# An adaLN block (state-space mixer and quantised feed-forward): decays in two half-chunk buffers, W_out in high and low parts, new orders

## The reference, cut to what matters

```python
zxbcdt = h @ W_in.T                          # z 1024, x 1024, B 128, C 128, dt 16
xBC = silu(conv4(xBC) + b_conv)
dt = softplus(dt_raw + dt_bias);  A = -exp(A_log)
# _ssd, per chunk, S is the state carried on:
L = exp(where(tril, cs[l] - cs[s], 0)) * tril       # cs = cumsum(dt * A)
Y_diag = (C B^T * L) X ;  Y_off = (C S) * exp(cs)
S = S * exp(cs_last) + B^T (X * exp(cs_last - cs))
y = (Y + Dp * X) * silu(z);  y = rmsnorm(y) * norm_w;  out = y @ W_out.T
# feed-forward: down(silu(gate(x)) * up(x)), weights (wq - 128) * scale
```

## Time and profile before

| what | us |
|---|---|
| median of 3 runs (1432.05 to 1432.34) | 1432.11 |
| profiled execution, span | 1430.4 |
| TensorE busy in it | 1408.2 (98%) |
| VectorE busy in it | 1143.5 (80%) |
| ScalarE busy in it | 641.9 (45%) |
| mixer and drain, until the feed-forward is alone | about 950 |

### The profile page before, as it was taken

How to read it: one execution, slowest core, us unless ns; L and a number is a source line. 1 busy time by engine, 2 the same in 40 slices (tenths; PEclk the granted TensorE clock), 3 DMA queues, 4 the chain that set the end, 5 groups by cost and what they waited for, 6 DMA issues and landing times.

```text
span 1430.4 us, 25660 instructions
## 1 busy us (share of the span) xinstructions
PE 1408.2 (98%) x9433; PEld 1134.0 (79%) x9433; DVE 1143.5 (80%) x2521; ACT 641.9 (45%) x1300; POOL 286.0 (20%) x335
## 2 busy tenths in 40 slices
PE   7999999999999999999999999899999999999998
PEld 3778787887887887887887887679888888888887
DVE  5799999999999999999999999856646546464542
ACT  5656566565565576476565565322202112020110
POOL 1012222223213213213212212221010211102101
PEclk9999999999999999999999999999999999999999
DMA  9413213213213213122222133612120201202010
GB/s 338 144 52 120 97 38 134 97 38 134 104 46 134 77 58 113 67 97 104 72 100 97 63 110 114 241 45 78 48 88 0 89 22 67 76 13 89 8 52 31
DMA packets 56411, 125.01 MB, mean 87 GB/s; under 512 B 6438, under 2 KB 10066, under 8 KB 52188
## 3 DMA queue, kind: packets, MB, share of 16 engines
q1 hardware_dynamic: 55744, 123.27, 24.2%
q10 hardware_dynamic: 540, 0.07, 0.0%
HBM read 97.62 MB, written 25.69 MB: 86 GB/s over the span
## 4 chain that ended last, share of the span: by engine, by line
PE 40%; DVE 37%; issue 15%; ACT 5%; DMA 1%; POOL 1%; DVEq 0%; POOLq 0%; SPq 0%; ACTq 0%
PE bank L2055 18%; DVE xBC L994 11%; PE bank L2085 9%; DVE decay L1069 6%; PE bank L1461 5%; DVE decay L1086 3%; DVE y L1142 2%; ACT decay L782 2%; DVE state L1129 2%; DVE X L1104 2%; PE bank L333 2%; DVE X_D L1135 1%; DVE y L1121 1%; PE bank L1617 1%; DVE bn_stats L965 1%
## 5 line engine op out<-in xcount | busy, mean ns | idle before, releaser
L994 DVE SCALAR_TENSOR_TENSOR xBC<-conv_in,wconv,xBC 128x256 f32<-128x256 f32 x480 | 240.8, 526 | 5.2 <-ACT xBC L709 4.3
L1890 ACT ACTIVATE silu_gate<-bank,params 128x512 f32<-128x512 f32 (+1 forms) x99 | 63.5, 642 | 372.0 <-PE bank L2055 352.5
L1962 DVE SCALAR_TENSOR_TENSOR hidden<-bank,params,silu_gate 128x512 f32<-128x512 f32 (+1 forms) x99 | 68.3, 690 | 129.2 <-PE bank L2055 124.1
L618 POOL TENSOR_TENSOR X_D<-X,Drow 128x1024 f32<-128x1024 f32 x32 | 65.7, 2052 | 388.1 <-ACT X_D L793 316.9
L2085 PE MATMUL bank<-W_down,hidden_high 128*128 128x512 f32 x374 | 138.9, 390 | 0.0
L2055 PE MATMUL bank<-ff_h_high,W_gate 128*128 128x512 f32 (+1 forms) x352 | 132.1, 379 | 0.0
L2055 PE MATMUL bank<-ff_h_high,W_up 128*128 128x512 f32 (+1 forms) x352 | 130.9, 376 | 0.4 <-DVE hidden L1962 0.4
L2055 PE MATMUL bank<-ff_h_low,W_gate 128*128 128x512 f32 (+1 forms) x352 | 130.9, 376 | 0.0
L2055 PE MATMUL bank<-ff_h_low,W_up 128*128 128x512 f32 (+1 forms) x352 | 130.9, 376 | 0.0
L2085 PE MATMUL bank<-W_down,hidden_low 128*128 128x512 f32 x330 | 128.4, 389 | 0.0
L1461 PE MATMUL bank<-h_high,W_in_high 128*128 128x256 f32 x640 | 126.5, 319 | 0.7 <-ACT z_dt L732 0.6
(11 more groups left out here) (194 smaller groups left out, 3183.9 us busy)
## 6 DMA issues: line engine op xcount, KB each, us to landing
decay<-sums_scratch SPq DMA_DIRECT2D x32, 1024.0 KB, 4.8
wq_rows<-wqT SPq DMA_DIRECT2D x33, 256.0 KB, 4.1
widened_scratch<-wq_rows SPq DMA_DIRECT2D x33, 256.0 KB, 2.0
x_tile<-x SPq DMA_DIRECT2D x32, 256.0 KB, 3.0
x_resid<-x SPq DMA_DIRECT2D x32, 256.0 KB, 2.8
x_scratch<-x_resid SPq DMA_DIRECT2D x32, 256.0 KB, 2.2
ff_x_resid<-x_scratch SPq DMA_DIRECT2D x32, 256.0 KB, 4.5
out<-ff_x_resid SPq DMA_DIRECT2D x32, 256.0 KB, 2.0
```

Of the source, the lines that this page charges most:

```text
L618: nc.gpsimd.tensor_tensor(A.XD[:].rearrange("p (h d) -> p h d", h=H), A.X[:].rearrange("p (h d) -> p h d", h=H), A.Drow[:].unsqueeze(2).br ...
L994: nc.vector.scalar_tensor_tensor(A.xc[b][:, m, :], A.raw[:, m, j:j + SC], A.wconv[:, m, j:j + 1], A.xc[b][:, m, :], ALU.mult, ALU.add).the ...
L1890: self.nc.scalar.activation(B.sg[m % 2][:, 0:size], self.gates[m % 2][:, 0:size], ACT.Silu, scale=self.T.sgate[:, m:m + 1]).then_inc(self. ...
L1962: nc.vector.scalar_tensor_tensor(hid, self.ups[m % 2][:, 0:size], self.T.sup[:, m:m + 1], B.sg[m % 2][:, 0:size], ALU.mult, ALU.mult).then ...
```

## The change

- Decays. One buffer `A.decay` in two halves `A.L[f]` of eight heads in the place of two chunk buffers. Each holds the heads f of chunk 0 and then of chunk 1. So the DMA for chunk 1 (`spread_sums`, 512 KB each) can be issued only when `y_diag(n, u, 0, f)` has read chunk 0, and `exp_decay(u, 1, f)` moves from the end of one turn into the middle of the next. In `drain` these DMAs are issued by ScalarE.
- `diff` is gone from VectorE. `exp_decay` makes it with eight `Relu(sum - x)` of 128x128 and then `Exp(-x)` on 1024 columns.
- W_out: `KF` = 7 tiles the split way and one plain. `evac_g` and `low_g` are made in two pieces each, `evac_g_last` copies the last tile.
- Work on a state that is zero (`fresh`: units 0 and 1, chunk 0) and on a state that nobody reads (`final`: units 14 and 15, chunk 1) is left out.
- Setup: the four matmuls of a section go to four groups of 32 columns of the array (`tile_position=(0, 32*k)`) without accumulation, and `turn_cols` adds the four groups by a matmul with `pick`.
- The orders of all engines are written anew; the residual of chunk 0 stands ahead of `rstd_next` on GpSimdE.

```diff
-        for k in range(self.T.DI // P - KH):
+        act.wait_ge(self.wout_in, 16 * (KF + 1))
+        for k in range(self.T.DI // P - KF):
...
-            mm = self.nc.tensor.matmul(self.mod_bank[s], self.A.sc[:, k, :], self.wm[s][:, k, :],
-                                       start=(k == 0), stop=(k == KD - 1))
+            g = self.GROUP * k
+            mm = self.nc.tensor.matmul(self.mod_bank[s][g:g + self.GROUP, :], self.wide_c[:, k, :], self.wm[s][k // 2][:, k % 2, :],
+                                       start=True, stop=True, tile_position=(0, g))
...
-            mm = self.nc.tensor.transpose(self.cols[s][:, k, :], self.mod_rows[s % 2][:, k * P:(k + 1) * P],
-                                          A.ident[0:2, 0:2])
+            mm = self.nc.tensor.matmul(self.cols[s][:, k, :], self.mod_rows[s % 2][:, k * P:(k + 1) * P], A.pick[:],
+                                       start=True, stop=True)
...
+    def fresh(u, c):
+
+        return u < 2 and c == 0
+
+    def final(u, c):
+
+        return u >= N - 2 and c == NC - 1
...
+    def spread_sums(queue, u, c, f):
+
+        if c:
+            wait(queue, ydiag_done, u, 2 * NC, f + 1)
+        else:
+            wait(queue, ydiag_done, u, 2 * NC, f + 1 - NC)
+        queue.dma_start(A.L[f].rearrange("p h l -> p (h l)"),
+                        T.cs_d[c].rearrange("h l -> (h l)")[f * HH * P:(f + 1) * HH * P]
+                        .rearrange("(a x) -> a x", a=1).broadcast_to([P, HH * P])).then_inc(cs_in[f], 16)
...
         def exp_decay(u, c, f):
+            wait(act, cs_in[f], u, 16 * NC, 16 * (c + 1))
+            if c == 0 and f == 0:
+
+                wait(act, sums_step, u, 3, 3)
+            x = A.L[f]
+            for h in range(HH):
+                o = c * H + f * HH + h
+                last = nc.scalar.activation(x[:, h, :], x[:, h, :], ACT.Relu, bias=A.s3[:, o:o + 1], scale=-1.0)
+            last.then_inc(diff_done, 1)
             wait(act, diff_done, u, 2 * NC, 2 * c + f + 1)
-            x = A.L[c][:, f * HH:(f + 1) * HH, :]
-            nc.scalar.activation(x, x, ACT.Exp).then_inc(decay_done, 1)
+            nc.scalar.activation(x, x, ACT.Exp, scale=-1.0).then_inc(decay_done, 1)
...
-            for h in range(f * HH, (f + 1) * HH):
-                last = nc.vector.tensor_scalar(A.L[c][:, h, :], A.L[c][:, h, :], A.s3[:, c * H + h:c * H + h + 1],
-                                               0.0, ALU.subtract, ALU.min)
...
-            for wp, gp in sorted(PARTS, key=lambda part: part[1]):
-                if gp == 1:
-                    wait(pe, glo_done, u, NC, c + 1)
-                for k in range(KH):
-                    nc.tensor.matmul(ps[:], gT[gp][:, k, :], Wo[wp][:, k, :],
-                                     start=(k == 0 and wp == gp == 0), stop=False)
+            halves = (range(0, 4), range(4, KF))
+            for f in range(2):
+                wait(pe, ghi_done, u, 2 * NC, 2 * c + f + 1)
+                for w in range(2):
+                    for k in halves[f]:
+                        nc.tensor.matmul(ps[:], A.gThi[:, k, :], Wo[w][:, k, :], start=(k == 0 and w == 0), stop=False)
+            for f in range(2):
+                wait(pe, glo_done, u, 2 * NC, 2 * c + f + 1)
+                for k in halves[f]:
+                    nc.tensor.matmul(ps[:], A.gTlo[:, k, :], A.Wohi[:, k, :], start=False, stop=False)
```

More of the change, by code:

```diff
@@ L67 @@
     ROWS = 3
+    GROUP = 32
     def __init__(self, nc, T, A, sem):
@@ L703, in evac_tile @@
             ps = a_wait(act, a_filled, n, ("m", m), 1)
+            if n == 0 and m == 0:
+                act.wait_ge(setup.mod_done, 2)
             wait(act, tail_step, n, 2, 0)
-            wait(act, yoff_done, before(n), 2 * NC, 0)
+            wait_for(act, yoff_done, yoff_count(before(n), 0) if n else 0)
             nc.scalar.activation(A.raw[:, m, 3:3 + SC], ps[:, 0:SC], ACT.Copy)
@@ L883, in turn @@
             if own:
-                silu_tile(n, b, 1)
+                evac_tile(n, b, 5)
+            if bef:
+                exp_decay(u, 1, 1)
+            if own:
                 evac_tile(n, b, 6)
@@ L1124, in decay_S @@
         def decay_S(u, b, c, f):
-            if u != N - 1 or c == 0:
-                wait(dve, yoff_done, u, 2 * NC, 2 * c + f + 1)
+            if not final(u, c) and not fresh(u, c):
+                wait_for(dve, yoff_done, yoff_count(u, 2 * c + f + 1))
                 wait(dve, e3_done, u, 1, 1)
@@ L1163, in low_g @@
+        def low_g(n, u, c, f):
+            wait(dve, ghi_done, u, 2 * NC, 2 * c + f + 1)
+            ps = t_wait(dve, t_filled, n, ("g", c, f), 1)
+            k = min(4 * f + 4, KF)
+            nc.vector.tensor_tensor(A.gTlo[:, 4 * f:k, :].rearrange("p k t -> p (k t)"), ps[:, 0:(k - 4 * f) * P],
+                                    A.gThi[:, 4 * f:k, :].rearrange("p k t -> p (k t)").bitcast(F32),
                                     ALU.subtract).then_inc(glo_done, 1)
@@ L1659, in turn @@
                 scores_G(n, u, b)
+                y_off(u, b, 0, 0)
             if own:
@@ L1694, in turn @@
                 transpose_g(n, u, 0, 0)
+                y_diag(n, u, 1, 0)
                 transpose_g(n, u, 0, 1)
+                y_off(u, b, 1, 0)
             if own:
@@ L1698, in turn @@
             if bef:
-                y_off(u, b, 1, 0)
-                y_diag(n, u, 1, 0)
                 y_diag(n, u, 1, 1)
@@ L1705, in turn @@
                 project_out(n, u, 0)
-                y_off(u, b, 1, 1)
             if own:
                 project_tile(n, 9)
+            if bef:
+                y_off(u, b, 1, 1)
+                states(n, u, 1, 0)
+            if own:
                 project_z(n, 0)
```

719 lines of the change are left out of this document (382 added, 337 removed).

## The result

The changed kernel takes 1415.99 us (median of 4 runs, 1415.06 to 1416.13) beside 1432.22 (1432.05 to 1432.51) on the same chip: a ratio of 0.9883, 95% interval 0.9869 to 0.9897. It is faster by 16.2 us, where 30.2 were forecast (1402, with a range up to 1414 for the rivals). The profiled execution spans 1414.3 for 1430.4.

A forecast was written before the change was run, and what follows sets the result against it. TensorE was taken as the bound. Savings of 13.1 up to turn 2, 14.7 in later turns, 3.4 left out and 1.0 drain, less 2.0 kept back, gave 30.2: 1402 us; range 1397 to 1407, with rivals 1396 to 1414.

The forecast's parts named there:

- W_out: Output projection on TensorE: three tiles moved to the split way save 0.48 us a chunk, 0.96 a turn.
- Work left out: Skipped `y_off` and `states` matmuls at 0.85 us each: 1.7 us saved in each of turns 1, 2 and 15.
- Decays on ScalarE: Relu at 0.28 us start to start, an `exp_decay` 3.3 us, ScalarE's sum 42.6 of 53.8 a turn, not the bound.
- rival 4: Relu and Exp may not share a table, so extra loads in each `exp_decay` cost 4.6 us a turn: 1471; chance 0.04.
- The new orders: Walk of a steady turn along the printed orders: TensorE stays fed, all covers hold by 0.4 to 1.3 us.
- rival 1: Thin covers fail in steady turns, tiles 5, 7 and 8 wait, one us in each of 15 turns: 1417; chance 0.14.
- Rival 5: On TensorE, waits or switches eat what the FR matmuls save, 15 us: 1417; chance 0.02.
- rival 2: Setup sections don't run side by side, the four in turn 0 cost 3.5 us as before: 1412; chance 0.10.
- Setup: Start and turn 0: cheaper sections bring turn 1's G to 56.2 us against 69.60, first projection at 18.6 for 19.93.
- Turn 1: TensorE stands about 5 us ahead of `y_diag(0,1)` for the late second decay block; turn 2 starts at 113.5 for 126.61.
- Rival 3: Turn 0 becomes bound by ScalarE or VectorE, 5 us more: 1407; chance 0.10.
- Drain: After the last turn: W_out saves 0.96 us, chunk 1's decays come late; bounds -2 to +3, only the 0.96 counted.

The follow-up runs named there:

- e9: e1 with `evac_tile(6)` moved between the Relu and the Exp of `exp_decay(1,1)` on ScalarE: 1407.5 us.
- e1: Changed kernel with `y_diag(0,1)` directly behind `y_diag(0,0)` and `y_diag(1,0)` moved to directly ahead of `y_diag(1,1)`, two half-width runs a turn: 1421.27 us.
- e2: Kernel before the change with its two runs of half-width matmuls broken where the changed kernel breaks them: 1441.68 us.
- e4: Changed kernel with 13 idle matmuls (zeros by zeros) added in TensorE's waits of the start: 1415.07 us.
- e6: Changed kernel with the first decay block's Relu ahead of `silu_z` 3, and `wout_scale` and `widen` behind the decays: 1419.6 us.
- e8: e3 with 12 idle F32 matmuls of 128 columns added behind `y_diag(0,0)` in turn 1: 1416.82 us.
- e10: e9 with e3's setup, 14 idle matmuls ahead of the first projection, `evac_x(0)` directly behind the decays and `widen` later: 1406.01 us.
- e5: Changed kernel with chunk 0's two `y_diag` joined and `y_diag(1,0)` behind `y_off(1,0)`, ahead of tile 8: 1412.45 us.
- e3: Changed kernel with setup sections 0 and 1 in the old form, summed in 2 rows with small transposes: 1414.1 us.
- e12: e10 with `widen` back at its old place ahead of silu 9: 1400.45 us.
- e7: Changed kernel with e3, e5's runs, e6's ScalarE order and idle matmuls in the setup and turn 1 together: 1412.67 us.
- e11: e3 with 10 idle F32 matmuls of 128 columns added ahead of `y_diag(0,0)` in turn 1: 1412.81 us.

## Why the prediction was half right

The time, 1402, was wrong by 14 us; W_out, the work left out, the decays and the sections' own price were right. Two steps failed. The steady turn was worked out as "54.83 - 0.96 - 0.09 = 53.78" from what leaves TensorE alone, and the price of a broken run, 0.61 to 0.63 a turn, stood at nothing. And of the setup the prediction counted a gain of 1.2, where the first projection came 2.9 us later than before, by TensorE's lower clock and a dearer `turn_cols`.

**W_out: right.** 0.48 a chunk forecast; 6.32 to 5.86 and 6.22 to 5.73 measured, 0.95 a turn for 0.96. The 0.09 for one switch less between F32 and FR was not seen: e9, whose runs are as long as the old ones, still needs 53.89, 0.1 above 53.78.

**Work left out: right.** Turn 15 lasts 52.90, 1.60 less than a steady turn, for 1.7.

**Decays on ScalarE: right.** A Relu lasts 393 ns and starts 0.29 behind the last (2.44 for eight); I took 0.28. The block takes 3.4 to 3.5 for 3.3, ScalarE's sum is 42.62 for 42.6. A turn has two table loads of 1.28, as before the change. One of them now stands between the Relu and the Exp of `exp_decay(n,0,0)`, where before the change it stood between the silu and the Exp; the other three blocks have none there (in turn 1 the second block's Relu run from 69.05 for 2.43 and its Exp starts at 71.52). So Relu needs no load of its own on either side, and rival 4 falls. VectorE came out at 46.65 for 47.

**The new orders: the walk held, its list of costs didn't.** The DMA of 512 KB landed in 4.3 us for the 4 taken. In turns 3 to 15 no tile waits for ScalarE, so rival 1 falls for the changed kernel; that its covers are real and thin is what e1 paid for (moving 1.09 us of `y_diag` away made tile 8 late by 0.97). The step that failed is the first one, "a steady turn should need 54.83 - 0.96 - 0.09": it counted what left TensorE and one kind of switch, and took the rest of TensorE's work as independent of order. I read the new order for waits and never for what stands next to what. Breaking two runs of half-width matmuls costs 0.61 to 0.63 a turn (e9, e2): 0.61 x 12 = 7.3 of the 7.9 us in the table. The earlier trace rows had the hint: its 64 records were one run, and the printed new order had `transpose_B(0)` in it. Rival 5 named the cause ("waits or switches eat what the FR matmuls save") but gave it 0.02 and the whole 15 us; what came took 0.6 of 0.96 a turn. The Trainium skill, "TensorEngine Tiling (Array Packing)", section "Key Properties", says that changing the tiling mode drains the TensorE; the trace agrees in so far as a run more takes some 0.3 us; a drain is not seen in it, and the page gives no price.

**A section side by side: right,** 1.00 us as taken, so rival 2 falls: four matmuls that share all their rows do overlap here, 1.00 for 3.48.

**Setup: wrong by 7.65.** The walk had the first projection at 18.6, tile 0 at 23.7 and G at 56.2; measured are 22.88, 29.23 and 63.85, so 4.3 were lost ahead of the first projection, 1.25 in zdt and 2.1 behind it. (1) "Of their gain I count 1.2" became a loss of 2.9: with short sections TensorE stood between the landings, its clock was at half until 28.3, and `turn_cols`, the transposes and zdt ran at half speed. By e4 that is 2.5 us ahead of the first projection; the whole of zdt at half is 1.2 more than in the kernel before, where a part of it was. Bounds of 0 and 3 had left a loss out, with no reason given. (2) `turn_cols` with a full matmul was taken at 0.1 more. It costs 0.81 to 0.99 at full clock, for 0.33, and 1.7 at half. Each has four F32 matmuls of 2 columns with a stationary operand of 128x128, in the place of four 2x2 transposes; that the loading of the large operand is what costs is likely, but no run shows it. Four of them at full clock are 3.53 us, 1.8 more than taken, and that is most of the 2.1 from tile 0 to G (34.6 for 32.5).

**Turn 1: right in size for a wrong reason.** 5 us of waits forecast, 0.86 + 1.46 + 2.75 = 5.07 measured. I had put them ahead of `y_diag(0,1)`, for the second block of decays; they stand ahead of the two zdt and `y_diag(0,0)`, the last for `evac_x(0)`. The wrong place cost e6 and e8. Turn 2's 1.5 us above the forecast are the 0.65 of the runs and a wait of 0.79 ahead of `y_diag(0,0)`. Rival 3 (turn 0 bound by ScalarE or VectorE) is not what happened: TensorE is busy for 40.84 of the 40.97 us of turn 0.

**Drain: a little better than forecast.** 2.7 gained with the feed-forward for 0.96. The waits of the drain add up to 3.3 (1.22, 0.88, 0.78, 0.42) for 4.5; the 2.7 lie within the bounds of -2 to +3. What shortened the waits was not tested.

The range, 1396 to 1414, missed by 2 us: the losses of rivals were taken one at a time, and here a small one in every turn and a larger one at the start came together.

## What to carry to other kernels

When an order is rewritten, list the neighbours as well as the waits: here a run of half-width matmuls had a price for each time it was broken, and it showed in the starts and not as idle time. Work taken from an engine that waits for data anyway gained little here (0.6 us of two sections), and on TensorE it cost the clock of what followed. Before a step is moved, ask who waits for what it stores: in e6 and e10 the same 0.6 us of `widen` cost 2 to 4 us through its store and SyncE's queue.

## What the hardware showed that was not expected

- One run of half-width matmuls more: 0.26 (e5) to 0.32 us (e2; e9 0.31, both half of two), and 0.35 between e5 and e9.
- TensorE's clock at the start: with a section of 3.19, two halves of 1.92 and waits between, half until 28.3 (in e9, with the same setup, one half-section took 1.05, at full clock, before it fell); with two sections of 5.45 and 3.53 back to back, full for the second and half again behind a wait of 3.51 (e3); with idle matmuls from 1.90 on, full at 7.98 (e4); with 14 of them ahead of the first projection, where the wait is then 0.18, full there too (e12, 0.50 from start to start).
- In turn 1 the granted clock fell to half for some 3 to 4 us in e3, e4 and e8, about a wait of 2.7 to 2.9, and for over 6 us in e6 and e7, about a wait of 5.1; not in e11, whose wait was 0.53. The changed kernel, e1, e5 and e9, with a wait of 2.75, were not slowed. What tells them apart was not found.
- A wait that the trace lays to VectorE (`scores`) was ScalarE's `evac_x`: where a matmul has several waits, the named one need not be the last.
